# Moving the roundings, the last step's row sums and three queue entries of a fused attention and int8 kernel

## What is computed

```python
def proj(W):
    y = jnp.einsum('oc,bct->bto', W, x)
    return y.reshape(B, T, H, Dh).transpose(0, 2, 1, 3)
Q, K, V = (proj(Wq), proj(Wk), proj(Wv))
att = jnp.einsum('bhqd,bhkd->bhqk', Q, K) * (1.0 / math.sqrt(Dh))
att = att + b[0]
m = mask[:, None, None, :]
att = att * m + (1.0 - m) * NEG_INF
att = jax.nn.softmax(att, axis=-1)
y = jnp.einsum('bhqk,bhkd->bhqd', att, V)
y = y.transpose(0, 2, 1, 3).reshape(B, T, C).transpose(0, 2, 1)
...
absmax = jnp.max(jnp.abs(y), axis=-1, keepdims=True)
scale = jnp.maximum(absmax, eps) / 127.0
q = jnp.clip(jnp.round(y / scale), -128, 127).astype(jnp.int8)
acc = jnp.einsum('bsk,nk->bsn', q, weight, preferred_element_type=jnp.int32)
out = acc.astype(jnp.float32) * scale * w_scale[:, 0] + bias
x = x + out.astype(jnp.float16)
```

## Time and profile before

| | us |
|---|---|
| median of 3 executions | 2300.28 (2298.8 to 2301.59) |
| the profiled execution | 2295.93 |
| its span | 2294.1 |
| TensorE busy | 2262.0 |
| VectorE busy | 1612.4 |
| ScalarE busy | 1541.7 |
| GpSimd busy | 1709.8 |

### The profile page before, as it was taken

How to read it: one execution, slowest core, us unless ns; L and a number is a source line. 1 busy time by engine, 2 the same in 40 slices (tenths; PEclk the granted TensorE clock), 3 DMA queues, 4 the chain that set the end, 5 groups by cost and what they waited for, 6 DMA issues and landing times.

```text
span 2294.1 us, 34646 instructions
## 1 busy us (share of the span) xinstructions
PE 2262.0 (99%) x11924; PEld 1359.3 (59%) x11924; DVE 1612.4 (70%) x2779; ACT 1541.7 (67%) x2681; POOL 1709.8 (75%) x735
## 2 busy tenths in 40 slices
PE   9999999999999999999999999999999999999998
PEld 7888888887555555555555555555555555555553
DVE  3311111118888888888888888888888888888882
ACT  4322222223788878878878888788878878787873
POOL 2322333322899988989999998999989898898995
PEclk9999999999999999999999999999999999999999
DMA  6665545575888888888888888888888888888874
GB/s 249 251 220 201 187 175 212 191 224 143 183 191 186 191 182 189 194 178 195 191 183 187 178 191 188 183 193 186 189 179 192 188 193 193 178 193 187 180 161 99
DMA packets 137909, 433.27 MB, mean 189 GB/s; under 512 B 12248, under 2 KB 48088, under 8 KB 113440
## 3 DMA queue, kind: packets, MB, share of 16 engines
q0 software_dynamic: 27360, 199.24, 43.1%
q1 hardware_dynamic: 101040, 205.85, 29.6%
q10 hardware_dynamic: 9360, 26.22, 3.7%
HBM read 130.06 MB, written 100.93 MB: 101 GB/s over the span
## 4 chain that ended last, share of the span: by engine, by line
PE 83%; issue 7%; POOL 4%; DMA 3%; ACT 2%; DVE 1%; POOLq 0%; ACTq 0%
PE score L798 18%; PE ring L147 17%; PE pv L829 16%; PE ring L344 11%; PE score L344 9%; PE ring L872 4%; DMA probs<-probs 3%; PE pv L344 3%; PE ring L839 2%; POOL acc L1176 2%; ACT probs L932 1%; POOL y L1183 1%; PE ring L862 1%; DVE absmax L1041 1%; DVE half_max L154 0%
## 5 line engine op out<-in xcount | busy, mean ns | idle before, releaser
L154 DVE TENSOR_REDUCE half_max<-ring 128x1 f32<-128x512 f32 x2048 | 1256.3, 677 | 68.7 <-PE ring L147 65.3
L932 ACT ACTIVATE probs<-score 128x512 f32<-128x512 f32 x2039 | 1037.7, 618 | 247.4 <-PE score L798 245.8
L1176 POOL TENSOR_TENSOR acc<-acc,probs 128x2048 f32<-128x2048 f32 x189 | 906.8, 4798 | 73.3 <-DMA probs<-probs 73.1
L798 PE MATMUL score<-q_stack,k_stack 100*128 100x512 f32 x2039 | 852.5, 419 | 0.4 <-ACT probs L932 0.4
L147 PE MATMUL ring<-k_stack,q_stack 98*128 98x512 f32 x2048 | 828.8, 405 | 16.6 <-DVE half_max L154 14.8
L798 PEld LDWEIGHTS score<-q_stack,k_stack 100*128 100x128 f32 x2039 | 386.2, 189 | 327.8 <-issue 191.7
L829 PE MATMUL pv<-probs,v_in 128*32 128x512 f32 x4096 | 493.7, 600 | 0.0
L147 PEld LDWEIGHTS ring<-k_stack,q_stack 98*128 98x128 f32 x2048 | 390.3, 191 | 112.1 <-DVE half_max L154 45.1
L1176 POOL TENSOR_TENSOR acc<-probs 128x2048 f32<-128x2048 f32 x63 | 297.4, 4720 | 43.5 <-DMA probs<-probs 37.2
L562 POOL TENSOR_TENSOR q_stack<-x_raw,k_stack 128x1024 fp32r<-128x1024 f32 x28 | 67.8, 2452 | 292.2 <-ACT k_stack L426 292.2
L829 PEld LDWEIGHTS pv<-probs,v_in 128*32 128x32 f32 x4096 | 107.1, 109 | 234.3 <-ACT probs L932 142.4
(11 more groups left out here) (118 smaller groups left out, 2112.9 us busy)
## 6 DMA issues: line engine op xcount, KB each, us to landing
probs<-probs POOLq DMA_DIRECT2D x190, 1024.0 KB, 8.4
q_stack<-qk_part SPq DMA_DIRECT2D x132, 256.0 KB, 4.2
k_stack<-qk_part SPq DMA_DIRECT2D x66, 512.0 KB
qk_part<-part_hi SPq DMA_DIRECT2D x64, 512.0 KB, 2.7
qk_part<-part_lo SPq DMA_DIRECT2D x64, 512.0 KB, 3.6
v_steps<-v_out SPq DMA_DIRECT2D x64, 256.0 KB, 2.3
v_in<-v_steps SPq DMA_DIRECT2D x32, 512.0 KB, 5.1
v_out<-x ACTq DMA_DIRECT2D x31, 512.0 KB, 5.3
```

Source lines behind the costliest of these rows:

```text
L154: nc.vector.tensor_reduce(half_max[:, pair // CHUNK, pair % CHUNK, half:half + 1], bank[:, :], AX_X, ALU.max, negate=True).then_inc(neg_ma ...
L798: pe.matmul(score[score_bank(s, t)][:, :], k_stack[par][0:ROWS, h, kt * P:(kt + 1) * P], q_stack[par][0:ROWS, half, h, :], start=True, sto ...
L932: nc.scalar.activation(probs[:, kt, h, :], score[score_bank(s, t)][:, :], ACT.Exp).then_inc(exp_done, 1)
L1176: nc.gpsimd.tensor_tensor(acc[:, half, :, :], first, probs[:, tile, :, :], ALU.add).then_inc(acc_done, 1)
```

## The change

Five things change in `attend`.

1. VectorE takes the maximum of half 0 at t = 27, ahead of `recip`, and not at t = 19; the maximum of half 1 and the scales at t = 43 and not at t = 39. ScalarE rounds in both instructions at t = 51.
2. ScalarE copies two heads of K at t = 27 and the third at t = 43, together with `double_q2(s + 1, 0)`, which stood at t = 35.
3. GpSimd does `add_bias(s - 2, 0)` and `add_residual(s - 2, 0)` ahead of `add(s - 1, 1, 1)` and not behind it.
4. In the last step VectorE adds the seven tiles 2 to 7 and 1 of half 1 into `acc[:, 1]` by six additions of 128 x 2048 elements (`add_last`; the first adds tiles 2 and 3, the others one tile each) at t = 47, 51, 55, 59 and, two of them, 63. One `sum_last` takes the place of `sum_tile`. VectorE's `scale_product(30, ...)` stands at t = 63 behind them.
5. In the last step the burst of t = 59 and `ffn(30)` move behind the scores of unit 63.

```diff
@@ -72,7 +72,9 @@
 USES = [(kind, t) for t in range(UNITS) for kind in ("max",) + EXTRAS.get(t, ())]
 PLACE = {use: i for i, use in enumerate(USES)}
 assert len(USES) % RINGS == 0
-ROUND, INTS = 43, 51
+SCALED, ROUND = 43, 51
+LAST_ADDED = {47: (3,), 51: (4,), 55: (5,), 59: (6,), 63: (1, 7)}
+LAST_ADDS = sum(len(tiles) for tiles in LAST_ADDED.values())
 SCORES = 3
 MAX_ROWS = 16
 GROUPS = 3 * TT
...
@@ -839,16 +842,12 @@
                     mm = pe.matmul(buf[h * DH:(h + 1) * DH, 0:N], ones[:, :], acc[:, half, h, :], start=True, stop=True)
                 mm.then_inc(sum_done, 1)
 
-            def sum_tile(tile, buf, start=False, stop=False):
-
-                if tile == PAIRS_OF_TILES[0][1]:
-                    pe.wait_ge(pair_done[0], 16 * QH * STEPS)
-                else:
-                    pe.wait_ge(exp_done, UNITS * LAST + GH * (TT + tile + 1))
+            def sum_last(buf):
+
+                pe.wait_ge(last_added, LAST_ADDS)
                 for h in range(GH):
-                    mm = pe.matmul(buf[h * DH:(h + 1) * DH, 0:N], ones[:, :], probs[:, tile, h, :], start=start, stop=stop)
-                if stop:
-                    mm.then_inc(sum_done, 1)
+                    mm = pe.matmul(buf[h * DH:(h + 1) * DH, 0:N], ones[:, :], acc[:, 1, h, :], start=True, stop=True)
+                mm.then_inc(sum_done, 1)
 
             def turn_q(s):
                 if isinstance(s, int) and s == 0:
@@ -880,7 +879,7 @@
                     if t == GH - 1 and prev:
                         for kt in (QH * TT - 2, QH * TT - 1):
                             weigh(s - 1, 1 - par, kt)
-                    if t % BURST == GH - 1 and t > GH:
+                    if t % BURST == GH - 1 and t > GH and (ahead or t != SUMS_0):
                         for kt in (t // GH - 2, t // GH - 1):
                             weigh(s, par, kt)
                     if t == TURN_1:
@@ -893,21 +892,17 @@
                         turn_q(s - 1)
                     if t == SUMS_0 and ahead:
                         sum_rows(s, 0, take_ring(s, ("sums", t)))
-                    if not ahead and t == UNITS - 13:
-                        last_sums = take_ring(s, ("sums", SUMS_0))
-                        sum_tile(2, last_sums, start=True)
-                    if not ahead and t == UNITS - 5:
-                        for tile in (3, 4, 5):
-                            sum_tile(tile, last_sums)
-                    if t == FFN and prev:
+                    if t == FFN and prev and ahead:
                         ffn(s - 1)
                     if not ahead and t == UNITS - 1:
+                        for kt in (QH * TT - 4, QH * TT - 3):
+                            weigh(s, par, kt)
+                        ffn(s - 1)
                         pe.wait_ge(prod_done, 2 * LAST - 1)
                         sum_rows(s, 0, ring_of(("ffn0", FFN)))
                         for kt in (QH * TT - 2, QH * TT - 1):
                             weigh(s, par, kt)
-                        for tile in (6, 7, 1):
-                            sum_tile(tile, last_sums, stop=tile == 1)
+                        sum_last(take_ring(s, ("sums", SUMS_0)))
                         for i in range(WARM_LAST):
                             pe.matmul(score[0][:, :], k_stack[par][0:ROWS, 0, 0:P], q_stack[par][0:ROWS, 1, 0, :], start=True, stop=True)
 
@@ -979,9 +974,10 @@
                     if prev and ahead and t == 19:
                         double_k(s + 1, 0)
                     if prev and ahead and t == 27:
-                        for h in range(1, GH):
-                            double_k(s + 1, h)
-                    if prev and ahead and t == 35:
+                        double_k(s + 1, 1)
+                        double_k(s + 1, 2)
+                    if prev and ahead and t == 43:
+                        double_k(s + 1, 3)
                         double_q2(s + 1, 0)
                     if t == GH - 1 and prev:
                         take_y(s - 1, 1)
@@ -995,7 +991,6 @@
                         double_q1(s + 2)
                     if t == ROUND and prev:
                         round_rows(s - 1)
-                    if t == INTS and prev:
                         make_ints(s - 1)
                         if s >= 2:
                             store_out(s - 2, 1)
@@ -1076,6 +1071,20 @@
                 dve.wait_ge(last_half_done, 1)
                 dve.wait_ge(res_loaded, 16 * STEPS)
                 nc.vector.tensor_tensor(res[:, N:2 * N], res[:, N:2 * N], half16[:, 1, :], ALU.add).then_inc(last_res_done, 1)
+
+            def add_last(tile, k):
+
+                if tile == PAIRS_OF_TILES[0][1]:
+                    dve.wait_ge(pair_done[0], 16 * QH * STEPS)
+                else:
+                    dve.wait_ge(exp_done, UNITS * LAST + GH * (TT + tile + 1))
+                if k == 0:
+                    dve.wait_ge(sum_done, 2 * LAST)
+                    first = probs[:, 2, :, :]
+                else:
+                    dve.wait_ge(last_added, k)
+                    first = acc[:, 1, :, :]
+                nc.vector.tensor_tensor(acc[:, 1, :, :], first, probs[:, tile, :, :], ALU.add).then_inc(last_added, 1)
 
             def take_qT(s):
                 dve.wait_ge(qT_done, s + 1)
@@ -1097,16 +1106,15 @@
                         join_max(nc, dve, half_max, neg_max, s, 1, neg_max_done, joined)
                     if t == GH - 1 and prev:
                         spread(s - 1, 0)
-                    if t == TURN_1 - 1 and prev:
-                        take_absmax(s - 1, 0)
-                        take_floor(s - 1)
                     if t == TURN_1:
                         low_max(nc, dve, ring_of(("turn", t)), max_parts, marks, s, 1, max_hi_done, max_lo_done)
                     if t == SUMS_1 and prev:
+                        take_absmax(s - 1, 0)
+                        take_floor(s - 1)
                         recip(s - 1, 1, ring_of(("sums", t)))
                     if t == SUMS_1 + 4 and prev:
                         spread(s - 1, 1)
-                    if t == ROUND - 4 and prev:
+                    if t == SCALED and prev:
                         take_absmax(s - 1, 1)
                         scales(s - 1)
                     if t == OWN + 2 * CHUNK - 1 and ahead:
@@ -1117,7 +1125,10 @@
                         take_qT(s - 1)
                     if t == SUMS_0 and ahead:
                         recip(s, 0, ring_of(("sums", t)))
-                    if t == FFN and prev:
+                    if not ahead:
+                        for tile in LAST_ADDED.get(t, ()):
+                            add_last(tile, sum(len(LAST_ADDED[u]) for u in LAST_ADDED if u < t) + LAST_ADDED[t].index(tile))
+                    if t == (FFN if ahead else UNITS - 1) and prev:
                         for half in range(2):
                             scale_product(s - 1, half)
 
@@ -1198,12 +1209,11 @@
 
             def step(s, par, prev=True, ahead=True):
                 second = not isinstance(s, int) or s >= 2
-                if prev:
-                    add(s - 1, 1, 1)
                 if second:
                     add_bias(s - 2, 0)
                     add_residual(s - 2, 0)
                 if prev:
+                    add(s - 1, 1, 1)
                     add(s - 1, 1, 2)
                 begin_pair(s, 0, 0)
                 if prev:
```

More of the change, by code:

```diff
@@ L626, in attend @@
         res_loaded = sem("res_loaded")
+        last_added = sem("last_added")
         k_doubled, q1_doubled, q2_doubled = sem("k_doubled"), sem("q1_doubled"), sem("q2_doubled")
```

## The result

The changed kernel takes 2310.49 us (median of 20 executions, 2293.95 to 2329.25), the kernel before 2300.41 beside it (20 executions, 2293.53 to 2306.0). The ratio is 1.0041 with a 95% interval of 1.0028 to 1.0054: slower by 10 us, where 24 us less had been forecast.

A forecast was written before the change was run, and what follows sets the result against it. TensorE was taken to bound quiet steps, GpSimd results asked for too early the others. Terms: -32 waits, -6 copies, +12 rounding, +4 last step = -22 us, giving 2273.9 or 2278.3; forecast 2276, range 2264 to 2287.

The forecast's parts named there:

- What bounds the kernel: TensorE bounds a quiet step of 52.7 us; GpSimd results asked for too early cause about 32 us of waits.
- Maximum and scales later: In each step, moving VectorE's maxima to t = 27 and 43 removes all 32 us of waits.
- the rival of waits that stay: GpSimd's reordered DMAs end later, so y comes later and half of the 32 us stays: 2292 us, chance 0.13.
- It sets no end of its own in the loop: GpSimd's reordered bias and residual, about 2.4 us, fill a DMA wait; GpSimd's later work comes 0 to 2.4 us earlier.
- makes certain that the maximum at t = 43 doesn't wait: GpSimd's new order ensures that VectorE's second row maximum does not wait; no separate gain was given.
- Two roundings at t = 51: On ScalarE, the exponential of unit 52 starts 0.4 us later each step: 12 us lost, bounds 0 and 1.3 a step.
- Copies: ScalarE's K copies: 0.2 us a step gained at t = 27, 6 us in all; nothing or 0.1 lost at t = 43.
- The last step: Six VectorE additions taking turns with GpSimd's outweigh the removed 3.79 us stop: 4 us lost.
- the row: Trace row in the projection: VectorE's two-input addition took 1.36 us beside GpSimd's, 0.69 alone, taken as mutual exclusion.
- the 0.9 us allowed for it: Last step: extra time if TensorE, idle for six microseconds, sums at half clock.
- the rounding pair: Rival at t = 51: exponential of unit 52 and late copies cost 1.8 us a step, 20 us slower: 2320; chance 0.05.
- The chance of 0.90 for faster: Whole kernel: the predicted probability of being faster by more than about 0.2% (4.6 us).

The follow-up runs named there:

- the best combination: Kernel before with GpSimd's new order, first maximum at t = 27, store at t = 47, load of x at t = 55: 2262.74 us, ratio 0.9838.

## Why the prediction was wrong

- **What bounds the kernel**: right. Quiet steps of 52.7 us and some 32 us of waits in 30 steps are what the best combination takes away (53.74 to 52.71 a step, 31 us).
- **Maximum and scales later: "I take all 32 us as gone."** Gone they are in the changed kernel with the early store, but the wrong part got the credit. Part 1 without part 3 leaves 0.55 us a step (order undone, 53.75 against 53.2) or 0.65 (maxima and roundings alone), about half, as the rival of waits that stay had it, though by another way. The order of GpSimd alone removes 0.67 of 1.03 us a step, 20 of the 31 us.
- **"It sets no end of its own in the loop"** and **"makes certain that the maximum at t = 43 doesn't wait"**: the step of the prediction that failed. It costed bias and residual as 2.4 us that fill a wait. It did not ask what the residual itself waits for, a load into a tile that a store must first empty, nor who stands behind it: `add(s - 1, 1, 1)`, whose tile the exponentials of t = 12 to 15 need. Those are the late steps.
- **The moved roundings**: the prediction counted the two instructions and not the DMA that is issued with them. `store_out` stands behind them on ScalarE. It came to be issued at 40.0 us of the step and not at 38.0, and that made the stops, together with the order of part 3: with the old order the mean step is 53.75 us with the late store (and the moved copies) and 53.77 with the early one (maxima and roundings alone), with the new order 54.6 and 53.2. Two DMAs on ScalarE's queue are in no term of the sum. With the store ahead of them the kernel takes 2285.95 us, inside the predicted range; the late store is worth +24.5 us at the median. The 42 us of the trace are those of the longest execution.
- **Two roundings at t = 51, +0.4 us a step**: right in place and size. The quiet step with part 1 alone is 53.1 us, with the old copies and the early store 53.1, against 52.7: +0.4, or 12 us. The prediction's own rows gave a little more, 1.25 - 0.76 = 0.49. In the changed kernel the exponential of unit 52 starts 41.1 us into the step where it was 40.6, and `high_max` as much later; 0.13 of that is the copies'.
- **Copies, -0.2 us a step**: the sign was wrong. The 0.3 us behind t = 29 go as foreseen, but "nothing, or 0.1" at t = 43 is 0.4, and the sum is +0.13 a step, +4 us and not -6. The two copies were set against the burst of 1.85 us (16 matmuls in the trace, and not 32), but they take 2.1. That ScalarE must catch up on its exponentials behind the burst as well is my reading; no run separates it.
- **The last step, +4 us**: right. From its start to the turn of the half 1 sums it was 2277.73 - 2217.1 = 60.6 us, and is 2311.07 - 2246.8 = 64.3: +3.6. The additions exclude GpSimd's, as the row had it:

```profile
2283.16 4.23 DVE L1087 TENSOR_TENSOR acc<-probs 128x2048 f32<-128x2048 f32 x1 [4.55 <-ACT probs L927]
2287.50 6.46 DVE L1087 TENSOR_TENSOR acc<-acc,probs 128x2048 f32<-128x2048 f32 x1
...
2294.48 9.46 DVE L1087 TENSOR_TENSOR acc<-acc,probs 128x2048 f32<-128x2048 f32 x4
2303.86 1.40 DVE L1097 SCALAR_TENSOR_TENSOR prod<-ring,scale,ws_rep 128x512 f32<-128x512 f32 x2
...
2311.07 0.72 DVE L1022 STREAM_TRANSPOSE sums_turned<-ring 128x512 f32<-128x512 f32 x1 [0.40 <-PE ring L849]
```

```profile
2280.08 5.15 POOL L1187 TENSOR_TENSOR acc<-acc,probs 128x2048 f32<-128x2048 f32 x1
...
2285.70 6.11 POOL L1187 TENSOR_TENSOR acc<-acc,probs 128x2048 f32<-128x2048 f32 x1
```

```profile
2304.66 1.94 PE L842 MATMUL ring<-acc,ones 128*32 128x512 f32 x8 [5.00 <-DVE prod L1097]
```

GpSimd's additions end at 2285.23 and 2291.81, and VectorE's, both begun before that, at 2287.39 and 2293.96: 2.15 us later both times, about the 2.29 that one takes alone. The row sum behind TensorE's wait of 5.00 us takes 1.94 and not 1.07, at a granted clock of 0.50 and not 1.00: the 0.9 us allowed for it. The +3.6 hides two larger terms, though. GpSimd's new order alone gives the last step 4.9 us (77.0 to 72.1), and against that parts 4 and 5 cost 8.6.

In sum, against the predicted 2276: +24.5 for the late stops at the median and +10 for the copies make 2310.5, which is what was measured. That it comes out to the decimal is luck, since the terms come from single executions of different lengths. Of the rivals none held. The slower one (the rounding pair, 2320) had the wrong mechanism and a chance of 0.05; that its time lies nearest to the measured one is luck as well. The chance of 0.90 for faster rested on every operation having been costed, and the two DMA issues had not been.

## What to carry to other kernels

When an instruction is moved or set in front of others, list every DMA issue that stands behind it on its engine's queue, and for each the transfer that it now meets and the one that waits for it. What is put into a wait at the head of a queue brings its own waits with it: name what it waits for, and what stands behind it. Where one producer is late, moving the consumers only moves the place at which it is felt; making the producer earlier (GpSimd, by moving two queue entries ahead of a third) gave 34 us at the median, where moving the consumers gave 5 with its costs in it.

## What the runs showed of the hardware

The same store takes 2.0 us or up to 8.5, and not the time in the step decides it but the distance behind GpSimd's last tile DMA. Over the twelve traces, 142 stores of steps 2 to 30 were issued less than 1.1 us behind it: 2.1 us to landing at the median, 135 of them at most 3.5, the other seven up to 8.5, which stays open. The 206 issued later landed without exception 0.2 to 2.8 us after that tile DMA had landed. With the early store and the new order 24 of 29 stand in the first group, in the changed kernel 10. With the late store and the old order only 7 do, but there the tile DMA is 4.7 us ahead at the median and nearly through. The landing lines of the load of `x`, before and after:

```profile
DMA to landing us min/median/max: 3.8/5.5/9.3
```

```profile
DMA to landing us min/median/max: 5.2/7.8/14.1
```

The exclusion of two-input additions works both ways: GpSimd's second one, begun at 2285.70 while VectorE's first ran until 2287.39, took 6.11 us and ended 4.42 after it. The Trainium skill (the page "SBUF — State Buffer", section "Who interferes with whom") says that the second to start is blocked fully; the 2.15 us with which each VectorE addition outlasts GpSimd's agree with it, and for which engine is served next when both have more to do, the rows show turns.
